# Second network of a fused graph kernel: the hi*lo score products are added on VectorE, and a bias seed is moved ahead of the exponentials

## What is computed

```
x = layernorm(x + L0(x, adj));   x = layernorm(x + L1(x, adj))
```

```
u     = einsum('bid,bjd->bij', h, h) / sqrt(384)
a     = softmax(u) ;  delta = a * adj ;  attn = delta / (sum(delta) + 1e-10)
hl, hr, hs = h @ wl.T + b_l, h @ wr.T + b_r, h @ ws.T + b_s
ctx   = (attn * upper) @ hl + diag(attn) * hs + (attn * lower) @ hr
h     = relu(layernorm(ctx) * g + beta)
```

## Time and profile before

| | |
|---|---|
| median of 3 runs | 1704.39 us |
| the profiled execution | 1703.78 us |
| its span | 1702.2 us |
| TensorE busy | 1665.3 us (98%) |
| VectorE busy | 1263.3 us (74%) |
| ScalarE busy | 955.2 us (56%) |
| GpSimd busy | 621.0 us (36%) |
| span that a steady pass takes | 104.27 us |

### The profile page before, as it was taken

One profiled execution on the slowest core, in us unless ns is written; L12 is line 12 of the kernel. 1 busy time (PEld: TensorE's weight loads), 2 busy tenths in 40 slices (PEclk: granted clock), 3 DMA queues, 4 the chain that ended last, 5 costly groups with the idle time before them and its releaser, 6 DMA issues.

```text
span 1702.2 us, 29769 instructions
## 1 busy us (share of the span) xinstructions
PE 1665.3 (98%) x9664; PEld 1577.8 (93%) x9664; DVE 1263.3 (74%) x2773; ACT 955.2 (56%) x2005; POOL 621.0 (36%) x668
## 2 busy tenths in 40 slices
PE   7999999999999999999999999999999999999995
PEld 6989889899898898988999999999999999999995
DVE  4587685876858677695887867769687696877866
ACT  4545456454553645546566665665655656656654
POOL 5143251432524334242532523425143351533505
PEclk9999999999999999999999999999999999999997
DMA  7015012020210203003103140400304004030111
GB/s 232 1 31 155 11 36 84 28 92 6 73 50 25 92 6 117 7 25 93 41 22 96 41 96 0 113 4 22 96 7 110 0 22 96 22 96 0 42 37 38
DMA packets 108008, 92.00 MB, mean 54 GB/s; under 512 B 63296, under 2 KB 101184, under 8 KB 107968
## 3 DMA queue, kind: packets, MB, share of 16 engines
q1 hardware_dynamic: 107968, 91.51, 18.8%
HBM read 66.33 MB, written 25.17 MB: 54 GB/s over the span
## 4 chain that ended last, share of the span: by engine, by line
PE 50%; issue 32%; POOL 11%; DVE 4%; ACT 1%; SPq 1%; DMA 0%; POOLq 0%; DVEq 0%; ACTq 0%
PE b_work L1175 34%; PE b_work L1188 6%; POOL g_qv_lo L624 3%; POOL b_ht L604 3%; PE b_work L372 2%; PE b_score_ps L119 2%; PE b_score_ps L386 1%; PE b_work L396 1%; POOL g_keep_l L619 1%; POOL g_sigma L633 1%; POOL g_a_nat L620 1%; PE b_turn L1132 1%; POOL g_frstd L637 1%; PE b_score_ps L1151 1%; DVE b_z L1694 1%
## 5 line engine op out<-in xcount | busy, mean ns | idle before, releaser
L1175 PE MATMUL b_work<-b_w_hi,b_ht 128*128 128x384 f32 x2304 | 605.6, 337 | 2.5 <-ACT b_work L1274 2.2
L1175 PEld LDWEIGHTS b_work<-b_w_hi,b_ht 128*128 128x128 f32 x2304 | 417.7, 188 | 4.0 <-ACT b_work L1274 3.9
L1175 PE MATMUL b_work<-b_w_lo,b_ht 128*128 128x384 f32 x1152 | 385.3, 334 | 0.0
L372 PE MATMUL b_work<-b_ht,b_w_hi 128*128 128x512 f32 x1152 | 357.8, 392 | 9.7 <-DVE b_w_lo L699 9.7
L624 POOL TENSOR_TENSOR g_qv_lo<-g_v_full,g_qv_hi 128x384 fp32r<-128x384 f32 x128 | 132.9, 1058 | 360.9 <-ACT g_qv_hi L495 360.9
L372 PEld LDWEIGHTS b_work<-b_ht,b_w_hi 128*128 128x128 f32 x1152 | 216.6, 189 | 51.3 <-issue 9.7
L372 PE MATMUL b_work<-b_ht,b_w_lo 128*128 128x512 f32 x576 | 226.1, 392 | 0.0
L1577 DVE TENSOR_TENSOR s_v_lo<-b_work,s_v_hi 128x384 fp32r<-128x384 f32 x256 | 139.3, 554 | 108.9 <-ACT s_v_hi L1280 107.9
L1175 PEld LDWEIGHTS b_work<-b_w_lo,b_ht 128*128 128x128 f32 x1152 | 216.5, 188 | 0.0
L731 DVE TENSOR_TENSOR g_qv_lo<-b_work,g_qv_hi 128x512 fp32r<-128x512 f32 x192 | 128.8, 687 | 110.5 <-ACT g_qv_hi L483 108.6
L396 PE MATMUL b_work<-b_w_hi,b_ht 128*128 128x384 f32 x768 | 206.2, 335 | 0.0
(11 more groups left out here) (164 smaller groups left out, 3259.5 us busy)
## 6 DMA issues: line engine op xcount, KB each, us to landing
b_x_in<-in_x_t SPq DMA_DIRECT2D x16, 768.0 KB, 7.3
g_x_res<-in_x SPq DMA_DIRECT2D x16, 768.0 KB, 7.6
b_x_in<-x SPq DMA_DIRECT2D x64, 192.0 KB, 6.7
s_x_res<-x SPq DMA_DIRECT2D x16, 768.0 KB, 7.0
out<-b_z SPq DMA_DIRECT2D x15, 768.0 KB, 4.1
x<-b_z SPq DMA_DIRECT2D x14, 768.0 KB, 3.9
b_a_tr<-in_adj_t SPq DMA_DIRECT2D x64, 64.0 KB, 3.3
g_a_nat<-in_adj SPq DMA_DIRECT2D x32, 64.0 KB, 2.4
```

The lines of the kernel that those rows point to most:

```text
L372: mm = pe.matmul(bank[:], w, h, start=(n == 0), stop=(n == len(pairs) - 1))
L1175: mm = pe.matmul(bank[:, 0:H], h, w, start=(n == 0 and side == 2), stop=(n == len(pairs) - 1), skip_group_check=True)
```

## The change

It does four things, all in the second network.

1. `fold_parts` no longer issues the two 256-column identity matmuls. The four of L1151 remain.
2. VectorE gets `whole_scores`: it waits for `folded`, adds `part` (128x512) to the scores in PSUM and signals a new semaphore, `score_whole`. It is issued in `begin`, after `variances` of the unit before and ahead of the maximum (L1793), and for the first unit ahead of its probabilities.
3. The exponentials of layer 0 and the maximum of layer 1 wait for `score_whole` instead of `folded`.
4. In `first_half` the exponentials move behind seed 3 (the fourth bias in order of jobs) and value_hi 0. The first unit's own order is left as it is.

```diff
--- before.py
+++ after.py
@@ -1025,7 +1025,7 @@
             sem("other_cut"), sem("other_summed"), sem("other_step"), sem("other_ready"))
         keep_ready = [sem(f"keep_ready{s}") for s in range(STREAMS)]
         work_full, work_free = sem("work_full"), sh.bank_free
-        part_copied, folded = sem("part_copied"), sh.folded
+        part_copied, folded, score_whole = sem("part_copied"), sh.folded, sem("score_whole")
         max_ready, bias_ready, sums_ready = sem("max_ready"), sem("bias_ready"), sem("sums_ready")
         exp_ready, exp_turned = sem("exp_ready"), sem("exp_turned")
         prob_ready, prob_hi_ready, prob_lo_ready = sem("prob_ready"), sem("prob_hi_ready"), sem("prob_lo_ready")
@@ -1144,9 +1144,6 @@
             def fold_parts(i, unit):
 
                 pe.wait_ge(part_copied, nth(i, unit, 1, 0))
-                for bank in (0, 2):
-                    pe.matmul(score_ps[:, bank:bank + 2, 0, :], eye_r[:], part[:, bank:bank + 2, :],
-                              start=False, stop=False, skip_group_check=True)
                 for t in range(NT):
                     mm = pe.matmul(score_ps[:, t, 0, :], part[:, t, :], eye_r[:], start=False,
                                    stop=(t == NT - 1), skip_group_check=True)
@@ -1251,7 +1248,7 @@
             def exponentials(i, unit):
 
                 if layer_of(unit) == 0:
-                    act.wait_ge(folded, nth(i, unit, 1, 0))
+                    act.wait_ge(score_whole, nth(i, unit, 1, 0))
                     nc.scalar.activation(raw[0], score_ps[:, :, 0, :], ACT.Exp, scale=SCALE).then_inc(exp_ready, 1)
                 else:
                     act.wait_ge(bias_ready, in_layer(i, unit))
@@ -1318,9 +1315,9 @@
             def first_half(i, unit):
                 seed(i, unit, 0)
                 seed(i, unit, 1)
-                exponentials(i, unit)
                 seed(i, unit, 3)
                 value_hi(i, unit, 0)
+                exponentials(i, unit)
                 value_hi(i, unit, 1)
                 seed(i, unit, 4)
 
@@ -1561,9 +1558,15 @@
                 nc.vector.transpose(flipped[k % 2].rearrange("p (b t) -> p b t", b=TOK // QUAD), flip_rows(sh, s, k))\
                     .then_inc(turned, 1)
 
+            def whole_scores(i, unit):
+
+                dve.wait_ge(folded, nth(i, unit, 1, 0))
+                nc.vector.tensor_tensor(score_ps[:, :, 0, :], score_ps[:, :, 0, :], part[:].bitcast(F32), ALU.add)\
+                    .then_inc(score_whole, 1)
+
             def maximum(i, unit):
                 done = in_layer(i, unit)
-                dve.wait_ge(folded, nth(i, unit, 1, 0))
+                dve.wait_ge(score_whole, nth(i, unit, 1, 0))
                 nc.vector.tensor_reduce(row_max[:], score_ps[:, :, 0, :], AX.X, ALU.max).then_inc(max_ready, 1)
                 dve.wait_ge(max_ready, done)
                 nc.vector.tensor_scalar(exp_bias[:], row_max[:], -SCALE, None, ALU.mult).then_inc(bias_ready, 1)
@@ -1790,6 +1793,7 @@
 
             def begin(i, unit):
                 variances(i, unit)
+                whole_scores(i, unit + 1)
                 if layer_of(unit + 1) == 1:
                     maximum(i, unit + 1)
 
@@ -1826,6 +1830,7 @@
                 final_normalise(i, s, count=0)
 
             gated.variances()
+            whole_scores(0, 0)
             probabilities(0, 0)
             dve.wait_ge(sh.next_small, 16 * 7)
             biased_value(0, 0, 0)
```

## The result

The changed kernel takes 1720.86 us (median of 4 runs, 1720.39 to 1722.11), where the kernel before took 1704.33 on the same chip: a ratio of 1.0098, with a 95% interval of 1.0086 to 1.011. It is slower by 16.5 us. The forecast was 1719.3, from 1706 to 1728. The span grew from 1702.2 to 1720.4 us, by 18.2.

What follows compares the result with a forecast made beforehand. TensorE, busy 98% of the span, was taken as the bound, with least reserve at ScalarE's bias seeds. 7 passes x (2.41 - 0.46) + 1.2 = +14.9 us on 1704.39 gave 1719.3 us, range 1706 to 1728.

Steps and rivals of the forecast that it cites:

- The removed matmuls, 0.23 us a fold: TensorE's fold: two matmuls fewer save 0.23 us a unit, at most 7.4 us over 32 units.
- Unit 0, +1.50 from v0 to v0: Layer 0: the fifth value product waits 1.31 us for its seed; 25.30 becomes 26.80 us between first value products.
- What would show it: Signs expected in the changed profile, among them TensorE idle 1.2 to 1.4 us before each layer-0 unit's fifth value product.
- Unit 1, +0.91: Second layer-0 unit: the fifth value product again waits for its seed; 26.52 us becomes 27.43.
- (c): Rival, layer 0: VectorE's lateness isn't paid back and the eighth value product waits too; 1727, up to 1732 us; chance 0.12.
- Layer-1 units: Units 2 and 3: nothing waits and the fold's gain is kept, -0.23 us each, -0.46 a pass.
- First pass, +1.2: First pass: unit 0 loses 1.9 us, units 1 to 3 gain 0.23 each, +1.2 us in all.
- (a): Rival: TensorE keeps the removed matmuls' gain, if seed(4) is over by 1273.1 in unit 0; 1697.0 or 1698.8 us; chance 0.11.
- (b): Rival: addition overlaps variances or handovers are shorter, fifth value product waits 0.3 to 0.7 us; 1701 to 1711; chance 0.09.
- (d): Rival: weight loads set the fold's spacing, so removing matmuls saves no TensorE time; 1723 us; chance within the forecast's 0.68.
- A clock that falls in the waits: Rival: TensorE's granted clock falls during the new waits, worse than all other rivals; chance 2 in 100, within (c).
- some 18 us in all: Expected total of TensorE's idle time before layer-0 units' fifth value products, where there were 2.2 us.

Runs made afterwards that it cites:

- e7: Changed kernel with the VectorE addition issued right behind the last context product, ahead of that tile's statistics and variances: 1699.33 us, ratio 0.9969.
- e5: Changed kernel with the two identity matmuls kept in the fold, so the products are added twice: 1724.44 us, ratio 1.0117.
- e4: Changed kernel, with GpSimd's diagonal product of unit 1 held back until VectorE's deviations are done: 1717.29 us, ratio 1.0073.
- e2: Changed kernel with the old ScalarE order, exponentials ahead of the fourth bias: 1755.06 us, ratio 1.0292.
- e10: e7 with the exponentials back in their old place, ahead of seed(3) and value_hi(0): 1722.97 us, ratio 1.0109.
- e3: Kernel before, with the whole change in layer-1 units only and layer 0 as it was: 1699.36 us, ratio 0.997.
- e6: Changed kernel with a second VectorE addition of the same size, into spare memory, ahead of the first: 1729.49 us, ratio 1.0148.

## Why the prediction was right, point by point

- **What bounds the kernel, and where it has no reserve** (the seeds): right. The waits of the value products for L1271 are the one item that grew, and e7 removes them in the steady passes by moving one instruction of 0.69 us.
- **The removed matmuls, 0.23 us a fold, kept in layer 1 and lost in layer 0**: right. Unit 2's row is 26.66 against a forecast of 26.67, and e5 gives 0.24. One handover differs: the fold of unit 0 now ends so early that its v0 waits for seed(0) (v0 came 0.58 after the fold's start, it was 0.40), so unit 3's row is 25.51 and not 25.34. The 0.17 is not extra, v4 of unit 0 has as much less to wait.
- **The addition, 0.69 us**: 0.70 measured. The Trainium skill, page VectorE: DVE Perf Modes, section on the TRN2 errata, gives (N+151)/0.96 ns for such an fp32 addition, 691 ns at 512 columns, and the trace agrees within 10 ns although two of the three operands are in PSUM.
- **Unit 0, +1.50 from v0 to v0**: +1.02 measured. The path from the end of variances to v4 was taken as 3.36 us and is 3.18 (1279.36 to 1282.54), since the step "1.71 us for all exponentials" was too long: in this profile value_hi(1) starts 1.49 after the raw exponential (1280.09 and 1281.58). The 1.71 ran to a seed(3) that, starting 0.04 after the context tile's end, had waited for VectorE and not only for the exponentials. With v0's 0.17 and 0.12 at the end of the unit that is the difference. So v4 came 0.87 us late and not 1.31, and the 1.2 to 1.4 us named under "What would show it" were not there. The place and the releaser are right, the size was forecast half as large again as it is.
- **Unit 1, +0.91**: +1.72 measured. The mechanism that I named is the right one, as e4 shows (27.46 against 27.43). That these agree to 0.03 us is partly luck: in e4 v4 comes 7.34 us behind v0 where the walk has 7.43, and the rest of the unit takes 20.12 where it has 20.00. What I did not have is the collision on L1659, 0.78 us a pass. I had walked ScalarE and VectorE of this unit up to v4 only and carried v7 over from unit 0, where it "just fits". Rival (c) had v7's wait, but for another reason, a debt that isn't paid back. VectorE does pay it back: contexts_out of unit 0 starts 25.12 us behind v0 (1300.42), 1.02 more than before and not 1.4 to 1.8.
- **Layer-1 units**: right, no wait. seed(4) starts 5.29 us after v0 (1335.15 and 1329.86), and the forecast had 5.26.
- **First pass, +1.2**: +0.4 measured (106.9 and 107.3 us from v0 to v0), and by other terms. Unit 0 loses 0.99 and not 1.9, unit 1 loses 0.37 where 0.23 was to be won, unit 2 wins 0.26 as forecast, and unit 3 wins 0.65, since the wait of 1.60 us at its v3 is gone with the move. The reading of the 2.2 us of seed waits had passed over that they are mostly this one. The trace shows the stall of unit 0 before v4, not at v6:

```profile
854.96 0.44 PE L1172 MATMUL b_work<-b_w_hi,b_ht 128*128 128x384 f32 x1 [0.71 <-ACT b_work L1271]
```

- **The total**: the errors are -0.48, +0.81 and +0.17 a pass and largely cancel. What is left of them, +0.5 a pass or 3.5 us in seven, is offset again by the 0.8 us of the first pass and by the profiled execution's being 1.3 us over the median. So the closeness of 1719.3 to 1720.9 is better than the working deserves: it is luck, while the mechanism is what the runs confirm.
- **The rivals**: (a) and (b) are out in this kernel, and (a)'s condition is just what e7 sets up: it comes to 1699.3, where (a) said 1698.8. (b) was nearer at v4 than in the sum, its 0.3 to 0.7 us against 0.87 measured. (d) is out, the matmuls' time goes (e5). A clock that falls in the waits: it stayed at 1.00 over the steady passes of the changed kernel, but in e2 and e10 it fell about the end of waits of 1.9 us and more. Two bounds were added up wrongly: (b)'s 14 x 0.3 gives 1706 and not 1701, and twice (c)'s 7.7 gives 1735 and not 1732. Neither moves the forecast.
- **TensorE's waits, "some 18 us in all"**: 17.2 in the page, which is luck as well. The forecast counted 1.31 a unit from start to start; the page's brackets leave out 0.17 each, v4's real wait is 0.87 in unit 0, and v7's wait in unit 1 fills the sum.

What stays open: the 0.1 us that unit 0 gains in e3, why unit 1 of the first pass loses 0.37 us, and why only some of e2's long waits came with a fall of the clock.

## What to carry to other kernels

Work handed to an engine with a quarter of its time free is not free: it costs what stands behind it in program order. Here an addition of 0.7 us in each of 32 units made the kernel 16.5 us slower, though the 16 units of layer 1 gained by the change. Before giving up such a change, look for the earliest place at which its inputs are ready; the same additions placed 1.4 us earlier in a layer-0 unit (the place behind the last context product at 1277.45 + 0.52 = 1277.97 instead of 1279.36 in the profile of the change) made the kernel 0.3% faster instead of 1% slower. When working out a wait from a timeline, count from start to start, and walk each kind of unit to its end, since a small shift can bring two other engines' instructions on top of each other. And look at the granted clock of each stretch before a difference is put down to the order of instructions alone.

## What the hardware showed that I had not expected

A VectorE instruction of 4 columns took 1.29 us instead of 0.15 because a GpSimd product of 128x512 had started 0.02 us ahead of it, and both ended together (0.02 apart, in the changed kernel and, with a part overlap, in e6). With the order turned round in e4 both have their normal lengths. The operands of both are in SBUF. The Trainium skill, page SBUF — State Buffer, section SBUF: two separate sides, has a rule that fits: VectorE and GpSimd share a pair of ports, a VectorE instruction with two SBUF inputs counts as a user of it against a GpSimd instruction that reads SBUF, and whichever starts first has it to its end. The runs agree with it, the loser being VectorE, but they show times and not ports. The addition itself has its scores in PSUM and only one input in SBUF. It overlapped a GpSimd instruction in all 32 instances of the changed kernel, and was 685 to 700 ns in each:

```profile
L1564 DVE TENSOR_TENSOR b_score_ps<-b_score_ps,b_part x32: 685/700/700, 849.6 to 1678.6; 128x512 f32<-128x512 f32 x32
```
